# Row sums of the one-headed graph attentions taken tile by tile beside the features, and the degrees of the scaled adjacency taken between the halves of layer 1's feed-forward stage

## What is computed

```
layer 0 gnn:  h = elu(gat(xn, W1, 8 heads of 768));  out = gat(h, W2, one head of 768)
layer 1 gnn:  h = elu(gat(xn, W1, 8 heads of 96));   out = gat(h, W2, one head of 768)
  gat:  f = x @ W;  s = sum_c f[:, c] * a_src[c];  t = sum_c f[:, c] * a_dst[c]      # row sums
        e = leaky_relu(s[src] + t[dst]);  e = exp(e - max over dst);  out = sum e * f[src] / sum e
layer 1 ffn:  rows 6..511:  gelu(x @ fc1) @ fc2
              rows 0..5 (class tokens):  two of five small "atom" networks, chosen by a gate
layers 2 and 3 gnn:  A = counts + I;  deg = column sums of A;  out = deg^-1/2 A deg^-1/2 (x @ W) + b
```

## Time and profile before

| what | value |
|---|---|
| median of three runs | 3429.54 us (3426.95 to 3431.44) |
| the profiled execution | 3425.07 us, its span 3422.9 us |
| PE busy | 3111.7 us, 91% |
| DVE busy | 1743.7 us, 51% |
| POOL busy | 1425.4 us, 42% |
| ACT busy | 749.5 us, 22% |
| HBM read | 253.67 MB, 75 GB/s |

### The profile page before, as it was taken

One profiled execution on the slowest core, in us unless ns is written; L12 is line 12 of the kernel. 1 busy time (PEld: TensorE's weight loads), 2 busy tenths in 40 slices (PEclk: granted clock), 3 DMA queues, 4 the chain that ended last, 5 costly groups with the idle time before them and its releaser, 6 DMA issues.

```text
span 3422.9 us, 39533 instructions
## 1 busy us (share of the span) xinstructions
PE 3111.7 (91%) x14175; PEld 2448.5 (72%) x14175; DVE 1743.7 (51%) x2919; ACT 749.5 (22%) x1315; POOL 1425.4 (42%) x1007
## 2 busy tenths in 40 slices
PE   8999798999999968989766789989999998989978
PEld 3576577888888855768645558768888886778857
DVE  7735698465555354347575455543333446741131
ACT  1044111233332222112133212121111112221222
POOL 2021288344434433645500025436666664436500
PEclk9999898999999989999978779999999999999986
DMA  2011365112212211222200132213323332113313
GB/s 79 19 47 38 111 208 188 51 56 75 65 56 63 76 56 44 85 68 74 83 0 9 42 97 74 74 58 95 98 87 101 96 92 74 59 51 101 92 48 111
DMA packets 91267, 256.99 MB, mean 75 GB/s; under 512 B 10335, under 2 KB 10975, under 8 KB 90852
## 3 DMA queue, kind: packets, MB, share of 16 engines
q1 hardware_dynamic: 80352, 219.45, 21.2%
q10 hardware_dynamic: 10788, 35.83, 3.0%
HBM read 253.67 MB, written 1.57 MB: 75 GB/s over the span
## 4 chain that ended last, share of the span: by engine, by line
PE 83%; DVE 10%; issue 3%; ACT 2%; POOL 1%; DMA 0%; DVEq 0%; ACTq 0%; POOLq 0%
PE ps L415 22%; PE ps L419 21%; PE ps L420 21%; PE ps L893 2%; PE ps L519 1%; DVE aux L1823 1%; PE ps L513 1%; PE ps L1000 1%; PE ps L1128 1%; PE ps L1031 1%; PE ps L772 1%; PE ps L783 1%; PE ps L765 1%; PE ps L757 1%; DVE hot L2172 1%
## 5 line engine op out<-in xcount | busy, mean ns | idle before, releaser
L363 POOL TENSOR_SCALAR w_hi<-raw 128x768 fp32r<-128x768 f32 x498 | 457.7, 919 | 1774.9 <-PE ps L415 1452.3
L366 POOL TENSOR_TENSOR w_lo<-raw,w_hi 128x768 fp32r<-128x768 f32 x498 | 976.0, 1960 | 41.5
L415 PE MATMUL ps<-H_hi,w_hi 128*128 128x512 f32 x804 | 318.8, 396 | 20.5 <-issue 15.5
L419 PE MATMUL ps<-H_lo,w_hi 128*128 128x512 f32 x804 | 316.7, 394 | 0.0
L420 PE MATMUL ps<-H_hi,w_lo 128*128 128x512 f32 x804 | 316.5, 394 | 0.0
L415 PE MATMUL ps<-B_hi,w_hi 128*128 128x512 f32 x720 | 291.8, 405 | 21.1 <-DVE B_lo L1619 14.9
L415 PE MATMUL ps<-A_hi,w_hi 128*128 128x512 f32 x780 | 307.8, 395 | 1.8 <-DVE sel_now L2094 1.8
L419 PE MATMUL ps<-A_lo,w_hi 128*128 128x512 f32 x780 | 304.7, 391 | 0.0
L420 PE MATMUL ps<-A_hi,w_lo 128*128 128x512 f32 x780 | 304.2, 390 | 0.0
L419 PE MATMUL ps<-B_lo,w_hi 128*128 128x512 f32 x720 | 283.3, 393 | 0.0
L420 PE MATMUL ps<-B_hi,w_lo 128*128 128x512 f32 x720 | 282.7, 393 | 0.0
(11 more groups left out here) (439 smaller groups left out, 5926.1 us busy)
## 6 DMA issues: line engine op xcount, KB each, us to landing
raw<-stream_dram SPq DMA_DIRECT2D x558, 384.0 KB, 3.1
w_ring<-w_dram ACTq DMA_DIRECT2D x39, 384.0 KB, 3.6
u_rows<-rows_dram ACTq DMA_DIRECT2D x8, 768.0 KB, 6.2
rows<-rows_dram ACTq DMA_DIRECT2D x7, 768.0 KB, 4.0
w_last<-w_dram ACTq DMA_DIRECT2D x9, 384.0 KB, 3.7
x<-x_dram ACTq DMA_DIRECT2D x1, 1536.0 KB, 9.7
out_dram<-x ACTq DMA_DIRECT2D x1, 1536.0 KB, 5.1
orf<-orf_dram ACTq DMA_DIRECT2D x6, 192.0 KB, 3.0
```

Source lines behind the costliest of these rows:

```text
L363: pool.tensor_scalar(w_hi[:, b // 3, b % 3], raw[:, b // 3, b % 3], 1.0, 1.0, ALU.mult, ALU.mult)\
L366: pool.tensor_tensor(w_lo[:, b // 3, b % 3], raw[:, b // 3, b % 3], w_hi[:, b // 3, b % 3], ALU.subtract)\
L415: mm = pe.matmul(o, wh, xh, start=first, stop=False, skip_group_check=True)
L419: pe.matmul(o, wh, xl, start=False, stop=False, skip_group_check=True)
```

## The change

It has three places. In layer 0, DVE takes the two row sums of a tile (against a_src and a_dst) right behind the add that completes this tile, ACT rounds tile by tile, and the four subtractions for B_lo stand behind `target_rows` instead of ahead of it. In layer 1, `features_n` calls `terms` for a tile ahead of its second subtraction. The two sums of a tile write to different scratch columns, so DVE waits for its own result once a tile rather than after each sum. In layer 1's feed-forward stage, PE makes the degrees between the up half and the down half; DVE makes the float counts ahead of the weighting, and copy, root, reciprocal, diagonal and scaled table directly behind it, ahead of the six `patches`.

```diff
@@ PE, ffn1
+                degrees()
                 pe.wait_ge(dve_to_pe, S.due(dve_to_pe))
                 for n in range(2):
...
                         whole_block_used()
-                        if (n, f) == (1, 0):
-                            degrees()
@@ ACT, gnn0
-                act.wait_ge(dve_to_act, S.due(dve_to_act))
...
                 for m in range(NT):
+                    act.wait_ge(dve_to_act, S.due(dve_to_act))
                     act.copy(bn[:, m], an[:, m]).then_inc(act_to_dve, 1)
@@ DVE
-            def features_n(marked=False):
+            def features_n(whole=None, marked=False):
...
                         dve.wait_ge(act_to_dve, S.due(act_to_dve))
+                        if g == 1 and whole:
+                            whole(m)
                         ins = dve.tensor_tensor(bn[1][:, m, c], sn[:, m, c], bn[0][:, m, c], ALU.subtract)
...
-            def terms(src):
-
-                dve.wait_ge(rows_in, S.due(rows_in, 16))
-                spare = edge_w[0][:, :, :].rearrange("p m n -> p (m n)")[:, 0:D]
+            def terms(src, m):
+
+                if m == 0:
+                    dve.wait_ge(rows_in, S.due(rows_in, 16))
+                spare = edge_w[0][:, :, :].rearrange("p m n -> p (m n)")
                 for r in range(2):
-                    for m in range(NT):
-                        S.step(dve.tensor_tensor_reduce(spare, src[:, m], rows[:, r], 1.0, 0.0, ALU.mult, ALU.add,
-                                                        nv[:, r, m:m + 1]))
-                    if r == 0:
-                        source_row()
-                mark(rows_free)
+                    ins = dve.tensor_tensor_reduce(spare[:, r * D:r * D + D], src[:, m], rows[:, r], 1.0, 0.0, ALU.mult, ALU.add,
+                                                   nv[:, r, m:m + 1])
+                S.step(ins)
+                if m == NT - 1:
+                    mark(rows_free)
@@ DVE, degrees
                 ins.then_inc(dve_to_pe, 1)
-                for j in range(KC):
-                    patches(j)
+
+            def scaled_counts():
+
                 dve.wait_ge(tile_for["dve"], S.due(tile_for["dve"]))
                 freed(dve.tensor_copy(row[:, :], ps[:, 0]), 0)
@@ DVE, gnn0
                         head_out(h, u)
-                mark(dve_to_act)
-                terms(accn)
+                        if h + 1 == GAT and u >= NT:
+                            mark(dve_to_act)
+                            terms(accn, u - NT)
+                source_row()
+                target_rows()
                 for m in range(NT):
                     dve.wait_ge(act_to_dve, S.due(act_to_dve))
                     dve.tensor_tensor(bn[1][:, m], accn[:, m], bn[0][:, m], ALU.subtract)
-                target_rows()
                 edge_weights()
@@ DVE, gnn1
-                features_n()
-                terms(sn)
+                features_n(lambda m: terms(sn, m))
+                source_row()
                 target_rows()
@@ DVE, ffn1
                 S.step(dve.memset(scr[:, 3, 0:80], 0.0))
+                degrees()
                 dve.wait_ge(act_to_dve, S.due(act_to_dve))
...
                 ins.then_inc(dve_to_pe, 1)
-                degrees()
+                scaled_counts()
+                for j in range(KC):
+                    patches(j)
                 dve.wait_ge(tile_for["dve"], S.due(tile_for["dve"]))
```

## The result

The changed kernel takes 3412.11 us (median of six runs, 3411.17 to 3417.15), the kernel before in the same sessions 3428.12: 16.0 us less by the medians. The ratio is 0.9959 with a 95% interval of 0.9949 to 0.9969, that is 14.1 us less (10.6 to 17.5). The profiled execution's span is 3410.2 us, 12.7 shorter than before. A second session gave 3414.36 and a ratio of 0.9965 (0.9951 to 0.9978). The forecast was 3411.7.

A forecast was written before the change was run, and what follows sets the result against it. PE, busy 91% of the span, bounds the kernel, and DVE sets the end only where PE waits, in three stretches. Gains of 7.8 + 3.7 + 6.3 = 17.8 us from 3429.5 give 3411.7, range 3404 to 3419.

The forecast's parts named there:

- Place A: End of layer 0's graph stage: row sums taken tile by tile let `target_rows` start earlier, 7.8 us gained.
- a pair beside POOL: Layer 0: a tile's two row sums take 3.6 us for three pairs meeting POOL's splitting, 2.5 for the other.
- Rival 2: Layer 0: a sum waits behind each POOL split, 4.9 a pair, gain 2.5 instead of 7.8; 3417.0; chance 0.13.
- rival 3: All three places: interference small and of the clock kind, gains 10.4, 3.7 and 10, 24 us; 3405.4; chance 0.17.
- The subtractions: Layer 0: four moved behind `target_rows`, 3.6 us in DVE's idle 4.57, cost nothing with 1.0 slack.
- Place B: Layer 1: row sums beside the features, POOL idle, `target_rows` at 1871.1 instead of 1874.78, 3.7 us gained.
- Place C: Layer 1's feed-forward stage: degrees moved between the halves, norm's sum at 2015.35 instead of 2021.71, 6.3 us gained.
- The two guessed clock edges: Layer 1's down half: clock rise put at 1983.5, fall at 2004.2, 6 us after the last wide product.
- the norm's first sum: Behind layer 1's down half: the norm's twelve passes took 7.58; a change of -1.7 to +3.8 put at zero.
- DVE's chain: Layer 1's feed-forward stage: copy, root, reciprocal, diagonals and scalings end at about 1990 and no longer decide.
- The sum: Whole kernel: 7.8 + 3.7 + 6.3 = 17.8 us gained, giving 3411.7.
- the rival for a slower result: Clock stays low from the degrees through down half and norm, +5 us, over 3436.4 if more runs half; chance 0.05.

The follow-up runs named there:

- `quiet`: Changed kernel, but PE reports six used weight blocks only after layer 0's last sums of exponentials, so POOL splits later; 3405.38 us, ratio 0.9933.
- `lo_ahead`: Changed kernel with the four subtractions for B_lo put back ahead of the target rows; 3416.66 us, ratio 0.9972.
- `c_only`: Kernel before with only the degrees moved between the halves of layer 1's feed-forward stage; 3425.86 us, ratio 0.9992.
- `early`: Changed kernel with degrees made behind the norm of layer 1's feed-forward stage, float counts ahead of layer 1's features; 3417.01 us, ratio 0.9965.
- `both`: Changed kernel with `quiet` and `early` together: later POOL splitting in layer 0 and early degrees; 3405.46 us, ratio 0.9939.

## Why the prediction was right

- **Place A, 7.8 forecast, 8.2 measured.** The step that carried it was the price of a pair beside POOL: 3.6 taken, 3.4 to 3.6 measured (0.95 and 2.58, 0.95 and 2.60, 1.84 and 1.56), and 2.5 for the third, in POOL's pause (0.95 and 1.57). The diagonal was put at 2.0 and took 2.15. `quiet` shows the cause: without POOL's splits the stretch is 4.4 instead of 10.25. Rival 2, 4.9 a pair, fell; rival 3's small interference too. Its bound with the last pair as before, 1244.4, is 1243.4 by its own terms (1236.37 + 0.56 + 3.6 + 0.7 + 2.2), so the gain of 10.4 in rival 3 should have been 11.4.
- **The subtractions, nothing forecast, nothing paid.** 1.10 us of slack was left, 1.0 forecast. `lo_ahead` prices the uncovered case at 3.5.
- **Place B, 3.7 forecast, 3.9 measured.**
- **Place C, 6.3 forecast, 5.5 at the norm's sum and 6.1 at DVE's centring.** The start of the down half was put 7.9 us behind the up half and came at 7.2. The two guessed clock edges were both too late, with opposite sign. The rise came 5.0 us behind the first degree product and not 10, while the degrees still ran (DVE's copy starts 6.2 us behind their start, where 6.85 + 0.27 was said), so the first turn took 16.8 instead of 17.8. The fall came 2.4 us behind the last wide product instead of 6, so five blocks and not 2.7 ran at half clock, 2.8 us more. The trace before held that price: its clock fell 5.0 us behind the degrees (2004.03 to 2009.03), but also 2.5 us behind the last wide product of the first turn (1996.28 to 1998.79), and the working used the longer one alone. That C came out within a microsecond is thus luck: errors of 0.7, 1.0 and 2.8 us nearly cancel. The 0.6 between 5.5 and 6.1 is the norm's first sum, put at zero: 7.00 for 7.58. DVE's chain ended at 1978.8, 15.2 behind the up half, where 16.5 was said (its own terms add up to 17.0). Its diagonals took 0.29 each rather than 0.55, since the shortest one in the trace before (0.47, at 2009.02) ran beside a split of POOL (2008.52 to 2009.35).
- **The sum, 17.8 forecast; 18.2 in the stretches, 14.1 (10.6 to 17.5) in the ratio.** The missing term is the 3.3 us in layer 3. The forecast said that the rest of the kernel is not touched, which holds for its instructions and not for its clock. It gave this a place only in the rival for a slower result. `c_only` shows that it eats half of C. The time itself, 3412.1 for 3411.7, is closer than the working deserves: it started from 3429.54 where the kernel before measured 3428.12 beside the changed one, and the second session gave 3414.36.
- **What stays open:** why the clock rises later there. It isn't a delay of 3.4 or 6.8 us, nor the order in the feed-forward stage alone (`early` against `both`). It goes with 0.1 us in the stage's distance from the clock's step before it, and how the new order moves that distance is not shown.

## What to carry to other kernels

Moving vector work beside other work is worth what it costs there, not what it costs alone: look at what GpSimd does in the new place, and whether the instruction has both inputs in SBUF. If the splitting of the next weights has slack, hold it back until the vector stretch on the path is over; that took 5.9 us off the stretch here, and 6.7 to 9.0 by the medians, where the whole change gave 12 to 16. Before taking wide products off the path, ask at which clock the ones behind them will start: here 6.2 us of products that stood where the clock was low were free. And look behind the edited stage, at stages that nothing was changed in: in `c_only` 3.3 of 6.2 us were given back there.

## What the runs showed of the hardware

- A row sum of 128 x 768 with both inputs in SBUF takes 0.95 us alone and up to 2.60 beside GpSimd's splitting, and the splits' 0.83 and 1.85 become 1.54 and 2.53; the adds with one input in PSUM keep their 0.56. That it goes this way is what the Trainium skill, page SBUF — State Buffer, "Who interferes with whom", says of two SBUF inputs, and the trace agrees. The times of place A add that the second waits until the first has ended.
- A busy PE did not keep its clock: in the second turn groups of twelve passes of 8 columns follow one another, PE is busy 16.53 of 17.00 us, and the granted clock is 0.50.
- In layer 3 the clock's rise came in one of two places, 8.3 to 8.4 or 11.6 to 11.7 us behind the stage's first product. It was the same place in both profiles of the changed kernel and in each pair of delayed ones, and 0.1 us in the distance from the clock's rise before the stage (up to 592.44 or from 592.51) goes with which.
